# Plain fp32 products in scores and values, squares summed on VectorE, and three moved steps in a linear-attention and selected-token layer

## What is computed

```python
xn = _layernorm(x, axis=-1)
x = x + _L0_attn_ref(xn, ...) + _L0_ffn_ref(xn, ...)
# first branch: 16 heads of 32 features, over blocks of the sequence
q = _silu(to_heads(q)); k = _silu(to_heads(k)); v = to_heads(v)
qkv_none_diag = jnp.einsum('bhmd,bhde->bhme', qi * q_decay, kv)
qk = jnp.einsum('bhmd,bhsd->bhms', qi, ki) * diag_decay
qkv_diag = jnp.einsum('bhms,bhse->bhme', qk, vi)
kv_new = block_decay * kv + jnp.einsum('bhsd,bhse->bhde', ki * k_decay, vi)
o = o * jax.lax.rsqrt(jnp.mean(o * o, axis=-1, keepdims=True) + EPS)
o = u * o
return o @ W_out.T
# second branch: the 256 tokens with the highest router scores
# 16 query heads of 128 on 8 key heads, rotary, causal softmax over 256, then a gated MLP of 2048
att = jnp.einsum('shd,thd->hst', q, kk) / np.sqrt(HEAD_DIM)
attn_out = jnp.einsum('hst,thd->shd', att, v).reshape(S, N_HEADS * HEAD_DIM) @ wo
mlp = jax.nn.silu(h2 @ w_gate) * (h2 @ w_up) @ w_down
```

## Time and profile before

| | us |
|---|---|
| median of 3 runs | 555.36 |
| lowest and highest | 554.13, 555.83 |
| the profiled execution | 554.96 |
| its span | 552.5 |
| PE busy | 513.8 (93%) |
| PEld busy | 472.6 (86%) |
| DVE busy | 333.8 (60%) |
| ACT busy | 256.0 (46%) |
| POOL busy | 241.8 (44%) |

### The profile page before, as it was taken

The page is one execution under the profiler, slowest core; times in us unless marked ns, Lnnn a source line. Parts: engine busy times, 40 slices in busy tenths (PEclk is TensorE's granted clock), DMA queues, the critical chain, the costliest instruction groups (busy, mean ns, idle before and its releaser), DMA issues. The chain is left out here.

```text
span 552.5 us, 11501 instructions
## 1 busy us (share of the span) xinstructions
PE 513.8 (93%) x4559; PEld 472.6 (86%) x4559; DVE 333.8 (60%) x647; ACT 256.0 (46%) x448; POOL 241.8 (44%) x207
## 2 busy tenths in 40 slices
PE   6978999999999999999998987889999799899984
PEld 6968899899999999989987976879988677799983
DVE  5977556763377887644437656899787545232331
ACT  8822233232256677422351426456767763554340
POOL 3022355242313432235257756544236124387983
PEclk9997999999999999999999988899999989999998
DMA  7813133202301011002405423545545632065522
GB/s 262 329 60 106 66 116 116 90 24 80 116 25 36 23 39 39 2 20 77 174 3 177 152 91 114 176 148 192 187 138 191 224 120 77 12 203 200 173 80 38
DMA packets 32884, 62.11 MB, mean 112 GB/s; under 512 B 3440, under 2 KB 3456, under 8 KB 32704
## 3 DMA queue, kind: packets, MB, share of 16 engines
q1 hardware_dynamic: 32288, 60.08, 32.5%
q0 software_dynamic: 544, 1.31, 1.2%
HBM read 48.27 MB, written 13.12 MB: 111 GB/s over the span
## 5 line engine op out<-in xcount | busy, mean ns | idle before, releaser
L1151 POOL TENSOR_TENSOR wlo<-raw,whi 128x512 fp32r<-128x512 f32 x96 | 129.7, 1383 | 106.3 <-ACT whi L525 106.2
L1215 PE MATMUL bank<-HTh,whi 128*128 128x256 f32 x224 | 64.6, 288 | 8.6 <-DVE rope L887 6.3
L1217 PE MATMUL bank<-HTh,wlo 128*128 128x256 f32 x224 | 64.1, 286 | 0.0
L1216 PE MATMUL bank<-HTl,whi 128*128 128x256 f32 x224 | 64.1, 286 | 0.0
L1132 POOL TENSOR_TENSOR state<-kv_new,state_dec 128x512 f32<-128x512 f32 x15 | 21.8, 1453 | 95.6 <-DVE kv_new L821 95.6
L810 DVE TENSOR_TENSOR A<-bank,DEC 128x512 f32<-128x512 f32 x64 | 39.7, 682 | 35.0 <-PE bank L1283 33.5
L525 ACT ACTIVATE whi<-raw 128x2048 fp32r<-128x2048 f32 x24 | 45.8, 1908 | 17.6 <-DMA raw<-in_w_down 12.5
L1215 PEld LDWEIGHTS bank<-HTh,whi 128*128 128x128 f32 x224 | 43.6, 195 | 10.0 <-issue 8.9
L1216 PEld LDWEIGHTS bank<-HTl,whi 128*128 128x128 f32 x224 | 43.6, 195 | 0.1
L1217 PEld LDWEIGHTS bank<-HTh,wlo 128*128 128x128 f32 x224 | 43.6, 195 | 0.0
L1261 PE MATMUL bank<-xTh,WKh 128*128 128x256 f32 x128 | 38.7, 303 | 2.3 <-DVE xTl L739 2.3
(11 more groups left out here) (283 smaller groups left out, 1560.1 us busy)
## 6 DMA issues: line engine op xcount, KB each, us to landing
X<-in_x SPq DMA_DIRECT2D x16, 256.0 KB, 3.4
xn_all<-XN SPq DMA_DIRECT2D x16, 256.0 KB, 2.8
uo_all<-uo SPq DMA_DIRECT2D x16, 256.0 KB, 2.7
raw<-in_wq SPq DMA_DIRECT2D x4, 1024.0 KB, 5.9
UR<-uo_all SPq DMA_DIRECT2D x16, 256.0 KB, 5.2
XR<-in_x SPq DMA_DIRECT2D x16, 256.0 KB, 3.0
out<-XR SPq DMA_DIRECT2D x16, 256.0 KB, 2.0
raw<-in_wo SPq DMA_DIRECT2D x4, 1024.0 KB, 5.9
```

The costliest lines, as they stand in the source:

```text
L1151: ins = Q.tensor_tensor(low[:, k, :], raw[b % 2][:, k, :], high[:, k, :].bitcast(f32), ALU.subtract)
L1215: T.matmul(dst, lh, rh, start=first, stop=False)
L1216: T.matmul(dst, lh, rl, start=False, stop=False)
L1217: return T.matmul(dst, ll, rh, start=False, stop=last)
```

## The change

Scores and values of both branches take plain fp32 operands: `score(N)` has 16 matmuls in the program instead of 48, a head's scores two instead of six, its values two instead of six. The splits of these operands go: kh and qh on ScalarE, ql on VectorE, kl on GpSimd for each chunk, and the high and low parts of the rotated queries and keys, of the values, and of the turned probabilities (PT). `rms` becomes one matmul on `sq_sum`, which a new VectorE reduction makes out of `sq` behind `mask`, and stands after the second tile instead of the first. The parked products are loaded with `load_uo(h + 3)`, and `load_uo(2)` ahead of the loop. `split_uo(0)` and `uo_low(0)` stand in chunk 15 instead of after it. At the end of the heads the order is out 13, out 14, transposes, out 15. The diff, cut to its core:

```diff
-        KRh, KRl = (at(n, kb, [P, FKV, SEL], f32r) for n, kb in (("KRh", 64), ("KRl", 72)))
+        KR = at("KR", 64, [P, FKV, SEL])
...
-        QRh, QRl = ([at(f"QR{i}{part}", kb, [P, 4, SEL], f32r) for i, kb in enumerate(homes)]
+        QR = [at(f"QR{i}", kb, [P, 4, SEL]) for i, kb in enumerate((112, 158, 96, 104))]
+        MTh, MTl = ([at(f"MT{i}{part}", kb, [P, 4, SEL], f32r) for i, kb in enumerate(homes)]
                     for part, homes in (("h", (112, 158, 96, 104)), ("l", (116, 162, 100, 108))))
 
-
-        kh, kl, qh, ql = (at(n, 112 + 2 * i, [P, NK, P], f32r) for i, n in enumerate(("kh", "kl", "qh", "ql")))
-        Vh, Vl = ([at(f"V{i}{part}", kb, [P, NS, DM], f32r) for i, kb in enumerate(homes)]
-                  for part, homes in (("h", (92, 124)), ("l", (120, 128))))
+        VA = [at(f"VA{i}", kb, [P, NS, DM]) for i, kb in enumerate((92, 124))]
...
+            load_uo(2)
             for h in range(STEPS):
-                if h + 2 < N_TILES:
-                    load_uo(h + 2)
+                if h + 3 < N_TILES:
+                    load_uo(h + 3)
                 if h < late_outs[0]:
                     store(h)
...
-            def k_high(N):
-                act.wait_ge(proj_sb, NPROJ * (N // CH) + 2)
-                act.wait_ge(s_ps, N), act.wait_ge(k_lo, N)
-                S.activation(kh[:], chunk(KT, N), ACT.Copy).then_inc(k_hi, 1)
-
-            def q_high(N):
-
-                act.wait_ge(proj_sb, NPROJ * (N // CH) + 4)
-                act.wait_ge(s_ps, N), act.wait_ge(q_lo, N)
-                S.activation(qh[:], chunk(QT, N), ACT.Copy).then_inc(q_hi, 1)
 
...
-                if N == -1:
-                    k_high(0)
-                    q_high(0)
-                if N >= 1:
-                    mean_square(N - 1)
-                if 0 <= N < N_TILES - 1:
-                    k_high(N + 1)
-                    q_high(N + 1)
                 count_marks(ranked(N, 0))
                 if N == -2:
                     weights_hi("V", v_w_hi)
...
                 in_position(N, 1, tiles)
+                if N >= 1:
+                    mean_square(N - 1)
                 if N == N_TILES - 2:
                     block_hi(2)
                 if N == N_TILES - 1:
                     block_hi(4)
+                    split_uo(0)
                 if N + XT_AHEAD < N_TILES:
...
+            def squares_summed(N):
+
+                dve.wait_ge(sq_ok, N + 1), dve.wait_ge(rms_ps, N)
+                V.tensor_reduce(out=sq_sum[:], in_=sq[:].rearrange("p k m -> p m k"), axis=mybir.AxisListType.X,
+                                op=ALU.add).then_inc(sum_sq, 1)
...
-                before = [v for v in range(u) if units[v][0][0] != "V"]
-                if n >= 2:
-                    dve.wait_ge(unit_hi, before[-2] + 1), dve.wait_ge(unit_lo, before[-2] + 1)
                 dve.wait_ge(unit_ps, u + 1), dve.wait_ge(cs_ok, 1), dve.wait_ge(part_in, 16 * 5)
                 if n:
-                    dve.wait_ge(staged_ok, n)
...
-                V.tensor_tensor(staged[:, n % 2, :].rearrange("p (a m) -> p a m", a=2), rope1[:], rope2[:],
-                                ALU.add).then_inc(staged_ok, 1)
-
-            def unit_low(u):
-                dve.wait_ge(unit_hi, u + 1)
-                src = job_bank("unit", u)[:] if units[u][0][0] == "V" else staged[:, (kq_count(u) - 1) % 2, :]
-                low_of(unit_dst(u, 1), src, unit_dst(u, 0), unit_lo)
+                V.tensor_tensor(unit_dst(u), rope1[:], rope2[:], ALU.add).then_inc(rope_ok, 1)
...
+                if N >= 1:
+                    squares_summed(N - 1)
...
-                if -1 <= N < N_TILES - 1:
-                    q_low(N + 1)
...
+                if N == N_TILES - 1:
+                    uo_low(0)
...
+            squares_summed(N_TILES - 1)
 
             dve.wait_ge(causal_ok, 3)
-            uo_low(0)
             for h in range(STEPS):
...
-                if 0 <= p < FH:
-                    dve.wait_ge(pt_hi, p + 1)
-                    if p >= 2:
-                        dve.wait_ge(ot_ps, p - 1)
-                    low_of(PTl[:, p % 2, :], B[4][:, 0:3 * P], PTh[:, p % 2, :], pt_lo)
...
-            def k_low(N):
-                pool.wait_ge(k_hi, N + 1)
-                Q.tensor_tensor(kl[:], chunk(KT, N), kh[:].bitcast(f32), ALU.subtract).then_inc(k_lo, 1)
-
...
-                pe.wait_ge(k_hi, N + 1), pe.wait_ge(q_hi, N + 1)
-                pe.wait_ge(k_lo, N + 1), pe.wait_ge(q_lo, N + 1)
-                pe.wait_ge(masked, 4 * N)
...
-                    for n, (k, q) in enumerate(((kh, qh), (kh, ql), (kl, qh))):
-                        for r in range(4):
-                            rows = slice(DH * r, DH * r + DH)
-                            ins = T.matmul(score_banks[r][:, j * P:(j + 1) * P], k[rows, j, :], q[rows, j, :],
-                                           start=n == 0, stop=n == 2)
+                    for r in range(4):
+                        rows = slice(DH * r, DH * r + DH)
+                        ins = T.matmul(score_banks[r][:, j * P:(j + 1) * P], chunk(KT, N)[rows, j, :],
+                                       chunk(QT, N)[rows, j, :], start=True, stop=True)
                 ins.then_inc(s_ps, 1)
 
             def rms(N):
 
-                pe.wait_ge(sq_ok, N + 1), pe.wait_ge(consts, 1)
-                for k in range(NK):
-                    ins = T.matmul(out_bank[:, 0:1], sq[:, k, :], mean1, start=k == 0, stop=k == NK - 1)
-                ins.then_inc(rms_ps, 1)
+                pe.wait_ge(sum_sq, N + 1), pe.wait_ge(consts, 1)
...
-                if N >= 1:
-                    rms(N - 1)
                 if N < N_TILES - 1:
                     keys_turned(N)
                 in_position(N, 1)
+                if N >= 1:
+                    rms(N - 1)
...
-                        ins = split_matmuls(B[h % 2][:, at:at + width],
-                                            (QRh[h // 4][:, h % 4, rows], QRl[h // 4][:, h % 4, rows]),
-                                            (KRh[:, kv, 0:width], KRl[:, kv, 0:width]), True, True)
+                        ins = T.matmul(B[h % 2][:, at:at + width], QR[h // 4][:, h % 4, rows], KR[:, kv, 0:width],
+                                       start=True, stop=True)
...
-                    split_matmuls(B[5][:, 0:SEL], (vh[:, 0, cols], vl[:, 0, cols]),
-                                  (PTh[:, g % 2, 0:SEL], PTl[:, g % 2, 0:SEL]), True, False)
-                    split_matmuls(B[5][:, P:SEL], (vh[:, 1, cols], vl[:, 1, cols]),
-                                  (PTh[:, g % 2, SEL:], PTl[:, g % 2, SEL:]), False, True).then_inc(ot_ps, 1)
+                    pe.wait_ge(value_ok, value_count(units.index((f"V{kv // 4}", 1))))
+                    pe.wait_ge(pt_ok, g + 1), pe.wait_ge(ot_lo, g)
+                    T.matmul(B[5][:, 0:SEL], VA[kv // 4][:, 0, cols], PT[:, g % 2, 0:SEL], start=True, stop=False)
+                    T.matmul(B[5][:, P:SEL], VA[kv // 4][:, 1, cols], PT[:, g % 2, SEL:], start=False, stop=True)\
...
-            for N in late_outs:
-                project_out(N)
+            project_out(late_outs[0])
+            project_out(late_outs[1])
             hidden_transposed(1)
+            project_out(late_outs[2])
```

91 lines of the change are left out of this document (34 added, 57 removed).

## The result

| | before | after |
|---|---|---|
| median, us | 555.60 (4 runs) | 521.99 (4 runs) |
| lowest and highest | 554.13, 556.56 | 521.71, 523.14 |
| the profiled execution, its span | 554.96, 552.5 | 522.22, 520.5 |

What follows compares the result with a forecast made beforehand. TensorE's list bounds chunks 2 to 13 and most of 1; later stretches are less clean. 17.1 + 1.3 + 1.2 + 16.2 + 0.3 - 7.5 + 5.1 = 33.7 us off 554.96 gives 521.3, forecast 521, range 512 to 534.5.

Steps and rivals of the forecast that it cites:

- TensorE's list in the chunks: Chunks: rms 0.65 us shorter 16 times, scores 0.45 us shorter in chunks 1 to 15; together 17.1 us gained.
- The heads' products: Heads: scores and values 0.66 us each, taking the upper bound of 0.22 us per 256-column pass; 1.2 us gained.
- rival 1: Heads: 256 columns of plain fp32 take 0.12 us a pass; 6.2 us more gain, 515 us; chance 0.11.
- rival 2: Chunk scores: row groups overlap only as a staircase, 1.8 us instead of 0.9; costs 13.4, 534 us; chance 0.09.
- rival 3: Chunk scores: row groups do not overlap at all, 3.6 us instead of 0.9; 561 us, slower; chance 0.05.
- The start: Chunk 0: of the 2.3 us wait for xTl, 1.3 us come back as the split copies go.
- Waits that go: Chunk 14 to the MLP: rope, parked product, OTl and pre-MLP waits removed, 1.5 + 4.5 + 3.4 + 3.0 + 0.6 + 3.2 = 16.2 us.
- Waits that come: V1 still waits about 2.3 us, 0.3 back; new waits at rms(15) and in head steps 0 to 3 cost 7.5 us.
- (c): Head steps 0 and 1: TensorE waits for out 0's bank, with out_rms late on GpSimd; some 3.0 us.
- (d): Head steps 1 to 3: VectorE, held by final(0), is still late with rope; 1.9 us.
- The clock: Half-clock stretches from 320 to 448 us cost 8.5 us; some go, two of 1.7 may come, net 5.1 back.
- Shifts as a whole: MLP behind the heads: its chain of loads, copies and low parts starts earlier and keeps its length.

Runs made afterwards that it cites:

- E1: Changed kernel with one part undone: rms multiplies the four squares on TensorE again, with no sum on VectorE; 529.17 us.
- E4: Kernel before with only the chunks' score product changed to plain fp32, the split copies still made but not used; 550.82 us.
- E3: Changed kernel with kh, qh, ql and kl of the chunks made again but not used, scores staying plain fp32; 527.01 us.
- E5: Changed kernel with split high and low operands restored for the heads' scores and values; 535.00 us.
- E11: Changed kernel with GpSimd's low parts ahead of the state, later rms for chunks 14 and 15, and sums, mean squares and unit 8's rope reordered; 518.28 us.
- E8: Changed kernel with parked product 0 split behind the chunks' loop again, as before; 522.18 us.
- E6: Changed kernel with parked products loaded two steps ahead in the heads, behind the step's block loads, as before; 524.28 us.
- E9: Changed kernel with chunk 15's sum ahead of its last unit's rope, and GpSimd's low parts ahead of the new state in chunks 13 to 15; 518.20 us.
- E7: Changed kernel with out 15 multiplied ahead of the transposes for the MLP, as before; 527.51 us.

## Why the prediction was right, and where its parts were off

It said 521 and the median is 521.99; the sum said 521.3 for an execution that took 522.22. The mechanisms of its large terms were right. Several sizes were not, and that they cancelled to within 1.7 us of the 33.7 is luck: up to out 13 alone the stretches below miss by -1.1, -1.7 and +2.9 us.

- **TensorE's list in the chunks.** Predicted 1.10 us a chunk; from chunk 1 to chunk 14 the distances fell by 13.4 us over 13, 1.03 each. `rms` was exact (0.66 in E1 for 0.65); the scores were over-sized (0.38 in E4 for 0.45). From the first start of chunk 5's scores to the next tile it is 128.83 - 127.73 = 1.10 us, and before it was 133.27 - 131.78 = 1.49 with the scores' start at 131.78: 0.39 for the four groups that went, priced at 0.45. The groups do come every 0.112 us and the last starts 0.22 us ahead of the tile in both kernels; but the gap between the first two is 0.21 us in plain fp32, where it was 0.16.
- **The reduction.** 1.06 us, in the range of 0.5 to 1.4, not the 0.69 that I took. It is hidden in every chunk but the last, as predicted, and there TensorE waited 2.40 us for 2.6 predicted. With kept split work (E3) the cover was gone: it was thin in the ranking chunks, which is what the prediction named as a way to be wrong.
- **The heads' products.** 0.65 us for scores and for values, predicted 0.66. The upper bound for 256 columns was the right one; rivals 1, 2 and 3 have nothing left: rival 1 needed 0.46 us, rivals 2 and 3 needed 1.8 and 3.6 us for a chunk's scores, which take about 1.
- **The start.** Predicted 1.3 us, measured 0.2 at chunk 1. The step that failed is that the wait for xTl is shortened by the copies that go. TensorE stood 6.0 us before its first projection tile there, where it had stood 3.7 and 1.9 us in two places: kl's wait only became part of xTl's. In the changed kernel and the nine made from it with plain scores (E1, E3, E5 to E11) chunk 1 starts anywhere from 59.2 to 61.8 us, so a gain of 1 us could not be seen in one profile anyway.
- **Waits that go.** The 1.5 us before unit 2 of chunk 14, the three of steps 2, 3 and 5 (shown by E5), the first parked product, the 3.0 near head 13 and the 3.2 before the MLP all went. Mis-sized: of the first parked product's 3.4, 1.9 come back as a wait in E8 and between 0.5 and some 2.2 us as time; the loads' 3.0 are shared with the heads' products, 1.2 for the loads in the changed heads (E6); of the short OTl waits half was to go, and they grew, from 1.2 to 2.2 us. The 3.2 before the MLP were right.
- **Waits that come.** V1 was right (2.54 us; I had said about 2.3). The same mechanism before V0, in chunk 14, 1.53 us, I missed: the low part of block 1 stands on GpSimd behind the state of chunk 13 and ends at 285.62 us, V0 starts at 285.72; when TensorE comes earlier, that queue doesn't. E9 shows it, by moving the low part ahead. Waits (c) and (d), 3.0 and 1.9 us predicted, were 0 and 0.69. Two things went into that. The half-clock stretch from 317 to 324 us lies on unit 8, which took 5.4 us instead of 3.1, and TensorE came later to what it would have waited for: in E6 and E7, which ran unit 8 at the full clock, there are rope waits of 1.3 and 1.5 us. But these 2.8 us are less than 4.9 as well. VectorE does wait there for `out_rms`, 1.7 us ahead of `final(0)` in E1, E6, E7 and E9, but TensorE meets that only at the rope operations behind it and not at the bank of out 0; of all kernels here only E11 has (c) itself. So (c) and (d) together were over-sized by 2.1 us, and by this comparison the slow clock hid another 2.1.
- **The clock.** Two stretches of 1.7 us of loss were predicted, one of 3.4 came; the net of 5.1 us was right, in part by luck, since E6, E7 and E8 have one of 1.7 and E9 none.
- **Behind the heads.** "Shifts as a whole" failed by 1.8 us. The MLP now has 3.1 us of waits, before 1.6. One that was not there before:

```profile
488.63 0.36 PE L1165 MATMUL bank<-HTh,whi 128*128 128x256 f32 x1 [1.20 <-ACT whi L514]
```

The copy ahead of it had waited 3.12 us for the transfer of an up block. The longest, 1.45 at 507.96 us, says "issue". ScalarE's waits for the transfers of gate and up blocks reach 3.2 and 3.1 us, where they were 2.0 and 2.3 before. It was not tried which order of loads or copies would remove that; E1 has 0.9 us of such waits and E7 3.0, and I have no account of the difference.

By stretches: 1.3 was predicted and 0.2 came up to chunk 1; 16.9 and 15.2 to chunk 15; 12.3 and 15.2 to out 13; 3.2 and 3.4 to the MLP; 0 and -1.8 behind it. These make 33.7 and 32.0 us (each rounded).

## What to carry to other kernels

Where one engine is full, count the records that a change takes off its list: those terms came out within 0.1 us a chunk. Where an engine waits, don't add up the waits that a change removes: a wait has the next late engine right behind it, and of 9.0 us removed in E9 4.2 came back in four others. Compare a wait between kernels at the same place in the program, not the longest of each. Give each queue (also ScalarE's and GpSimd's) the same look as the one that you relieve, because its work keeps its place behind a state or a mean square when the rest comes earlier.

## What was new on the hardware

- A reduction over the middle axis, 512 fp32 elements read with a stride into 128, took 1.06 us on VectorE, half as long again as a product of 512 elements (0.69).
- Plain fp32 products of 32 rows on four row groups overlap like split ones: 32 records in 1.17 us. "TensorE: Matmul & The Clock Gate" of the Trainium skill, section "Part 3: Packing small matmuls — row/col tiling", says that matmuls never overtake one another; the records don't contradict it, four start within 0.02 us of each other and the next four 0.11 us later, but the staircase that rival 2 drew from it is not in the trace.
- Plain fp32 costs two passes of 0.11 us for 128 columns and two of 0.22 for 256: a head's two products of each kind are 0.65 us. "FP8 and Floating Point Precision" of the Trainium skill, section "TensorE Precision Notes", counts four passes; in time the trace agrees (0.44 us for 256 columns, for 0.12 of one fp32r product), in records it shows two for each product.
- The place of a half-clock stretch differed between kernels that waited the same: behind the same wait of 2.40 us E6 and E7 ran at the full clock, with 3.4 us of half clock at the end of the wait before it (2.55 and 2.53 us), and the changed kernel had 6.8 us of it. The difference of 3.4 us at half clock is 1.7 us of time.
